# A graph attention layer: VectorE takes its V weights from SBUF, and the last sum moves to the last norm

## The chip, the cores and the metric

The kernel runs on one core of one Trainium2 chip. The metric is the device time of one execution in microseconds. Runs of this kernel lie within about 0.1% of each other; a change of 0.2% is about what a measurement can tell from none.

## The reference

4096 nodes with 512 features, 131072 edges with 8 biases each. One layer of attention along the edges, a feed-forward part, and a last norm over input plus layer:

```python
z = ln(x)*g1 + b1
q, k, v = z@Wq + bq, z@Wk + bk, z@Wv + bv          # 8 heads of 64
scores = (q[src] * k[dst]).sum(d) * scale + bias    # an edge and a head
alpha  = softmax of scores over the edges of one src
att    = sum over those edges of alpha * v[dst]
x1 = x + att @ Wo + bo
z  = ln(x1)*g2 + b2
y  = silu(z @ W1 + c1) @ W2 + c2                    # 512 -> 1024 -> 512
out = layernorm(x + x1 + y)
```

## The kernel before, in words

**First phase** (until about 1470 us): q, k, v are computed for all nodes and written to HBM, the edges are sorted into records by source node (GpSimd scatters 1024 times 128 records), and nodes are ranked by their number of edges. It isn't touched.

**Second phase.** 32 tiles of 128 nodes each, the nodes with most edges first. A tile's edges are worked off in groups of 8 slots: a slot holds one edge of each of the 128 nodes. A tile has 3 groups or more: most tiles have 5, later 4, the last ones 3, and there are 145 groups in all. In the code `stage` 0, 1 and 2 are the first three groups of a tile, stage 3 is every further one. A group goes so:

- GpSimd gathers K and V of its 8 slots from HBM with 8 indirect DMAs (L527, 512 KB each) into one of three buffers of the ring `region_a`. Before each pair of slots it waits until the weighting of that pair, three groups before, has released the buffer (`V_READY`). SyncE waits for the landings and passes them on (`LANDED`, L368).
- VectorE multiplies K by q, in four instructions of two slots (L1016, `products`); TensorE sums over d with transposes (L1356), ScalarE copies (L699), TensorE folds (L1364) into the scores.
- VectorE adds the bias, takes the running maximum and subtracts it (L1062 to L1066, `softmax`).
- ScalarE takes the exponents (`exponents`): L710 those of slots 2 to 5 into PSUM (`pv_ps`), L711 all of them into SBUF (`pr`).
- V is weighted: slots 2 to 5 by VectorE in two instructions (L1027, `weigh`), which read V from SBUF and the weights from `pv_ps`; slots 0, 1, 6 and 7 by ScalarE, a head at a time (L727). TensorE sums the weighted V with transposes (L1374), ScalarE copies (L705), TensorE turns that back into the accumulator (L1384), which VectorE scales (L1035).

VectorE weights group g after the products of group g+1, and ScalarE weights slots 6 and 7 of group g at the start of group g+1, ahead of that group's exponents.

Between the groups the tail of earlier tiles is woven in, in an order written out by hand. In tile t: in stage 0 VectorE adds the residual and norms tile t-2 (`middle`, L1114 to L1125), and TensorE computes the second feed-forward product of tile t-3 (`down`, L1423); in stage 1 VectorE adds that sum to the residual of tile t-3 (`take_y`, L1082), and TensorE does the first half of the first product of t-2 (`up`, L1415); in stage 2 VectorE takes the last norm of tile t-3 (`last_norm`, L1087 to L1094), TensorE the second half of `up` and the output projection (L1399) of tile t-1. Stage 0 also copies the new tile's q into PSUM (L1131). After the last tile the remaining steps are written out one after another.

PSUM has eight banks. `y_ps`, where `down` sums, is the first of the two banks of the hidden values (`h_ps[0]`), so `up` waits until `take_y` has emptied it:

```python
h_ps = bank[5:7]
y_ps, pv_ps = h_ps[0], bank[4][:, 0:(GROUP - 4) * HEADS].rearrange("p (s h) -> p s h", h=HEADS)
```

Each engine works off its own instructions in order; they meet by semaphores alone. GpSimd, VectorE, ScalarE, TensorE and SyncE each run their own loop over tiles and groups.

Of the kernel before, what the change touches and what calls it, by code (L numbers as in the profile page):

```python
# [36 lines left out]
def layer_kernel(nc, x, src, dst, edge_bias, Wq, bq, Wk, bk, Wv, bv, Wo, bo, ln1_g, ln1_b,  # L37
# [37 lines left out]
    with ExitStack() as ctx:  # L75
# [138 lines left out]
        qkv_ps = [bank[3], bank[4], bank[3]]  # L214
        scT_ps, sc_ps = bank[0][:, 0:2 * P], bank[0][:, 2 * P:2 * P + 2 * SH]
        vT_ps, acc_ps = bank[1], bank[7]
        wo_ps, q_ps = turn_ps, bank[3]
        h_ps = bank[5:7]
        y_ps, pv_ps = h_ps[0], bank[4][:, 0:(GROUP - 4) * HEADS].rearrange("p (s h) -> p s h", h=HEADS)

        names = """kv00 kv01 kv02 kv03 kv10 kv11 kv12 kv13 kv20 kv21 kv22 kv23 more_loaded rec_loaded src_loaded edges_loaded weights_loaded consts_a pad_ready
            table_cleared bias_cut bias_out bias_in hist_in hist_turned keys_ready turned turned_sb turned_out onehots_free onehots_ready hist_done prefix_in
# [399 lines left out]
        def _(act):  # L622
# [84 lines left out]
            def exponents():  # L707

                act.wait_ge(S["sc_ready"], now)
                act.activation(pv_ps, sc[:, 3:GROUP - 1, :], ACT.Exp)  # L710
                act.activation(pr[:, 0:GROUP + 1, :], sc[:, :, :], ACT.Exp).then_inc(S["p_ready"], 1)  # L711
                act.drain()

# [88 lines left out]
        def _(dve):  # L802
# [218 lines left out]
            def weigh():  # L1021

                kv_in = slots(was)
                dve.wait_ge(S["p_ready"], groups)
                for s in range(2, GROUP - 2, 2):
                    dve.wait_ge(SUMMED[s // 2], groups)
                    dve.tensor_tensor(vw[:, s:s + 2, :].rearrange("p s (h d) -> p s h d", h=HEADS),  # L1027
                                      kv_in[:, s:s + 2, C:2 * C].rearrange("p s (h d) -> p s h d", h=HEADS),
                                      pv_ps[:, s - 2:s, :].unsqueeze(3).broadcast_to([P, 2, HEADS, D]),
                                      ALU.mult).then_inc(V_READY[s // 2], 1)  # L1030

            def scale():
# [43 lines left out]
            def summed(reg):  # L1076
                return s_all[:, bass.ds(dve.snap(reg, min_val=0, max_val=C), C)]

            def take_y(k, s_w):

                dve.wait_ge(S["y_done"], k + 1)
                dve.tensor_tensor(s_w, s_w, y_ps[:, :], ALU.add).then_inc(S["y_taken"], 1)  # L1082
                dve.drain()

            def last_norm(u, s_w):

                dve.bn_stats(stats[:, :], s_w)  # L1087
                dve.drain()
                dve.bn_aggr(mv[:, 2:4], stats[:, :])
                dve.drain()  # L1090
                inverse_root(1)
                dve.tensor_copy(out_idx[:, :], row_all[:, u, 0].bitcast(I32))
                dve.tensor_scalar(s_w, s_w, mv[:, 2:3], rstd[:, 1:2], ALU.subtract, ALU.mult)
                dve.drain().then_inc(S["out_ready"], 1)  # L1094
# [33 lines left out]
            def body(t, stage):  # L1128
# [16 lines left out]
                    weigh()  # L1145
                    dve.tensor_copy(sc[:, 0, :], m_run[:, :])
                if stage == 1:
                    with dve.If(t > 2):
                        take_y(dve.snap(oldest), summed(dve.snap(dve.snap(q_at) * -1 + C)))
                    with dve.If(t > 0):  # L1150
                        finish(t)
                    first_weights()
                    dve.drain()
# [37 lines left out]
                if stage == 2:  # L1191
                    with dve.If(t > 2):
                        other = dve.snap(dve.snap(q_at) * -1 + C)
                        last_norm(bass.ds(dve.snap(nc.s_assert_within(t - 3, 0, NT - 4, skip_runtime_bounds_check_because="the If has t > 2")), 1),
                                  summed(other))
                    dve.nop()

# [15 lines left out]
            def half(u):  # L1213
                return s_all[:, (u % 2) * C:(u % 2 + 1) * C]
# [2 lines left out]
            middle(NT - 1)  # L1217
            hold(S["out_sent"], 16 * (NT - 3))
            residual(half(NT - 2))
            take_y(NT - 2, half(NT - 3))  # L1220
            dve.reg_add(groups, groups, 1)
            finish(NT)
            silu(NT - 1, 0)
            last_norm(slice(NT - 3, NT - 2), half(NT - 3))
            silu(NT - 1, 1)
            middle(NT)
            hold(S["out_sent"], 16 * (NT - 2))
            residual(half(NT - 1))
            take_y(NT - 1, half(NT - 2))
            last_norm(slice(NT - 2, NT - 1), half(NT - 2))  # L1230
            silu(NT, 0)
            silu(NT, 1)
            hold(S["out_sent"], 16 * (NT - 1))
            take_y(NT, half(NT - 1))
            last_norm(slice(NT - 1, NT), half(NT - 1))

        @block.tensor
        def _(pe):
# [169 lines left out]
            def up(k, a):  # L1408

                if a == 0:  # L1410
                    pe.wait_ge(S["z2_sb"], k)
                    pe.wait_ge(S["y_taken"], k)
                for m in range(a * HT // 2, (a + 1) * HT // 2):
                    for c in range(KT):
                        last = pe.matmul(h_ps[m // 4][:, (m % 4) * P:(m % 4 + 1) * P], W1_sb[:, c, m * P:(m + 1) * P],  # L1415
                                         z2T[:, c * P:(c + 1) * P], start=c == 0, stop=c == KT - 1)
                last.then_inc(H_DONE[a], 1)

            def down(k, a):

                pe.wait_ge(H_READY[a], k)
                for m in range(a * HT // 2, (a + 1) * HT // 2):
                    last = pe.matmul(y_ps[:, :], hT[:, m * P:(m + 1) * P], W2_sb[:, m, :], start=m == 0, stop=m == HT - 1)  # L1423
                if a == 1:
                    last.then_inc(S["y_done"], 1)
# [102 lines left out]
```

## Time and profile before

| what | value |
|---|---|
| median of 3 runs | 3608.19 us (3605.18 to 3608.59) |
| profiled execution | 3609.14 us, span 3607.4 us |
| PE busy | 2811.9 us (78%) |
| VectorE (DVE) busy | 2631.0 us (73%) |
| GpSimd (POOL) busy | 2342.4 us (65%) |
| ScalarE (ACT) busy | 1695.5 us (47%) |
| gathers L527 | 1160, 998 ns each |
| ScalarE's weighting L727 | 4640, 336 ns each |
| products L1016 | 580, 1216 ns each |
| VectorE's weighting L1027 | 290, 1213 ns each |

The share of busy time is a mean over phases with different limits; the time outside the second phase is 1470 of 3607 us. A gather's time on GpSimd is the time to issue it; its data lands later. In the timeline an "x4" row merges instructions of one kind that follow each other, and the bracket is the idle time of that engine ahead of the row with what ended it; "issue" there is time in which the engine waited for nothing that the profile shows.

### The profile page before, as it was taken

What the parts mean: (1) busy time and instruction counts of PE and PEld (TensorE: products, weight loads), DVE (VectorE), ACT (ScalarE), POOL (GpSimd) and SP (SyncE); (2) the same over time, 40 slices, a digit from 0 to 9 for tenths busy, and PEclk for the clock granted to TensorE, in tenths of its full rate; (3) what the DMA queues carried; (4) which work ended last, traced back from release to release, by engine and by line L of the source; (5) the groups of instructions that cost most, each with busy time, mean ns of one, the idle gap of its engine ahead of it and who ended that gap; (6) DMA issues with size and microseconds to landing.
All of it is one profiled execution on the core that took longest, in us unless ns stands there. A gap on an engine that the chain in (4) does not pass through costs nothing.

```text
span 3607.4 us, 82722 instructions
## 1 busy us (share of the span) xinstructions
PE 2811.9 (78%) x18693; PEld 2155.2 (60%) x18694; DVE 2631.0 (73%) x6460; ACT 1695.5 (47%) x6541; POOL 2342.4 (65%) x2549
## 2 busy tenths in 40 slices
PE   8665666666566666487888889988889898988997
PEld 7433333333333333377777777777777777777775
DVE  9777667767667766376777777777777777777874
ACT  0111111111111111286777777777777776777774
POOL 0477777777777777676666666666666666666650
PEclk5666666776667777698999999999999999999999
DMA  7323232323232222877888788788688888888770
GB/s 291 86 79 91 77 82 75 79 79 89 79 82 75 78 78 73 307 270 248 306 299 277 268 294 297 258 282 309 234 289 280 294 280 296 276 291 276 247 280 24
DMA packets 285668, 719.24 MB, mean 199 GB/s; under 512 B 86900, under 2 KB 103476, under 8 KB 285383
## 3 DMA queue, kind: packets, MB, share of 16 engines
q0 software_dynamic: 211776, 585.54, 47.3%
q1 hardware_dynamic: 73862, 133.41, 11.9%
q14 instruction: 23, 0.18, 0.0%
q8 instruction: 7, 0.11, 0.0%
HBM read 717.02 MB, written 72.97 MB: 219 GB/s over the span
## 4 chain that ended last, share of the span: by engine, by line
PE 36%; POOL 18%; issue 18%; DVE 8%; ACT 7%; DMA 6%; DVEq 3%; ACTq 2%; POOLq 1%; SPq 0%; PEld 0%; PEldq 0%
POOL records L410 17%; PE bank L1356 13%; ACT region_c L727 7%; PE wide L1415 6%; PE wide L1423 6%; DMA records<-region_c,pos_i 6%; PE bank L1399 3%; PE wide L1374 3%; DVE region_c L1016 2%; PE bank L1255 2%; PE wide L1384 2%; DVE region_c L964 1%; ACTq L727 1%; POOL region_a L527 1%; ACTq L766 1%
## 5 line engine op out<-in xcount | busy, mean ns | idle before, releaser
L527 POOL DMA_INDIRECT region_a<-kv,cols x1160 | 1157.8, 998 | 535.0 <-issue 434.0
L410 POOL DMA_INDIRECT records<-region_c,pos_i x1024 | 1010.8, 987 | 445.3 <-issue 412.7
L727 ACT ACTIVATE region_c<-region_a,pr 128x64 f32 x4640 | 1155.5, 336 | 44.0 <-issue 44.0
L1016 DVE TENSOR_TENSOR region_c<-region_a,bank 128x1024 f32<-128x1024 f32 x580 | 670.5, 1216 | 88.9 <-issue 61.0
L1356 PE MATMUL bank<-ident,region_c 128*128 128x128 f32 x4640 | 613.5, 289 | 129.9 <-DVE region_c L1016 124.9
L1356 PEld LDWEIGHTS bank<-ident,region_c 128*128 128x128 f32 x4640 | 584.5, 197 | 155.8 <-issue 150.0
L1374 PE MATMUL wide<-ident,region_c 128*128 128x128 f32 x4640 | 566.9, 275 | 78.0 <-ACT region_c L727 78.0
L1374 PEld LDWEIGHTS wide<-ident,region_c 128*128 128x128 f32 x4640 | 514.4, 144 | 111.9 <-ACT region_c L727 111.8
L649 ACT COPY region_c<-region_a 128x64 f32 x128 | 32.5, 254 | 1063.0 <-DMA records<-region_c,pos_i 1063.0
L1313 PE MATMUL bank<-region_b,region_a 128*128 128x512 f32 x768 | 490.7, 798 | 0.0
L1313 PEld LDWEIGHTS bank<-region_b,region_a 128*128 128x128 f32 x768 | 189.6, 260 | 253.3 <-issue 253.3
L1027 DVE TENSOR_TENSOR region_c<-region_a,bank 128x1024 f32<-128x1024 f32 x290 | 339.9, 1213 | 1.1 <-issue 1.1
L1300 PEld LDWEIGHTS wide<-region_c 64*128 64x128 f32 x2048 | 167.3, 241 | 239.9 <-issue 239.9
L928 DVE SCALAR_TENSOR_TENSOR region_c<-region_a,region_c 128x128 bf16<-128x128 int16 x1024 | 292.4, 349 | 24.1 <-issue 24.1
L1300 PE MATMUL wide<-region_c 64*128 64x64 f32 x2048 | 185.7, 335 | 152.4 <-issue 152.4
L699 ACT COPY region_c<-bank 128x256 f32<-128x256 f32 x145 | 54.0, 372 | 463.0 <-PE bank L1356 463.0
L1415 PE MATMUL wide<-region_c,region_b 128*128 128x128 f32 x2048 | 239.2, 275 | 3.2 <-ACT region_c L737 3.2
L1415 PEld LDWEIGHTS wide<-region_c,region_b 128*128 128x128 f32 x2048 | 233.6, 192 | 3.7 <-ACT region_c L737 3.7
L1423 PE MATMUL wide<-region_b,region_c 128*128 128x512 f32 x512 | 225.0, 592 | 0.0
L946 DVE TENSOR_TENSOR pos_i<-region_c 128x8 int32<-128x8 f32 x128 | 21.5, 168 | 271.1 <-DMA records<-region_c,pos_i 266.1
L1320 PE MATMUL bank<-ident,region_a 128*128 128x128 f32 x128 | 35.7, 434 | 228.2 <-DVE region_a L960 228.2
L1255 PE MATMUL bank<-region_c 128*64 128x64 bf16 x2048 | 180.3, 318 | 1.7 <-DVE region_c L847 0.7
(185 smaller groups left out, 3206.2 us busy)
## 6 DMA issues: line engine op xcount, KB each, us to landing
region_a<-srcT SPq DMA_DIRECT2D x128, 256.0 KB
region_a<-kv,cols POOLq DMA_INDIRECT x1160, 5.8
region_a<-hiT SPq DMA_DIRECT2D x256, 64.0 KB
records<-region_c,pos_i POOLq DMA_INDIRECT x1024
x_rows<-region_c SPq DMA_DIRECT2D x32, 512.0 KB
kv<-region_a SPq DMA_DIRECT2D x32, 512.0 KB
records<-region_c SPq DMA_DIRECT2D x32, 480.0 KB, 14.8
region_a<-in_x_dram SPq DMA_DIRECT2D x32, 256.0 KB
```

The costliest lines, as they stand in the source:

```text
L410: pool.indirect_dma_start(records, bass.IndirectOffsetOnAxis(ap=pos_i[j % 2][:, s:s + 1], axis=0), rec_w[j % 2][:, s, :], None).then_inc(S ...
L527: pool.indirect_dma_start(KV[r][:, s, :], None, kv, bass.IndirectOffsetOnAxis(ap=cols[r][:, s:s + 1], axis=0), bounds_check=L - 1, oob_is_ ...
L727: last = act.activation(vw[:, s, of], v_part[:, s, C + hd * D:C + (hd + 1) * D], ACT.Copy, scale=pr[:, s + 1, hd:hd + 1])
L928: last = dve.scalar_tensor_tensor(eq[:, s * P:(s + 1) * P], srcb[b][:, s * P:(s + 1) * P], src_f[:, bass.ds(st * STREAMS + s, 1)], tri[:, ...
L1016: last = dve.tensor_tensor(prods[:, of, :], kv_in[:, of, 0:C], q_ps[:, :].unsqueeze(1).broadcast_to([P, 2, C]), ALU.mult)
L1027: dve.tensor_tensor(vw[:, s:s + 2, :].rearrange("p s (h d) -> p s h d", h=HEADS), kv_in[:, s:s + 2, C:2 * C].rearrange("p s (h d) -> p s h ...
L1300: last = pe.matmul(wide_ps[b][:, side, s * LO:(s + 1) * LO], hitT[b][rows, s * P:(s + 1) * P], table_sb[rows, s * LO:(s + 1) * LO], start= ...
L1313: last = pe.matmul(qkv_ps[w][:, :], zT1[:, c * P:(c + 1) * P], Wqkv[:, w, c, :], start=False, stop=c == KT - 1)
L1356: last = pe.matmul(scT_ps[:, a * P:(a + 1) * P], prod_cols[:, i, a * SH:(a + 1) * SH], ident[:, :], start=i == 0, stop=i == D // FOLD - 1, ...
L1374: last = pe.matmul(vT_ps[:, c * P:(c + 1) * P], vw[:, s, c * P:(c + 1) * P], ident[:, :], start=s == 0 and c == 0, stop=s == GROUP - 1, is ...
L1415: last = pe.matmul(h_ps[m // 4][:, (m % 4) * P:(m % 4 + 1) * P], W1_sb[:, c, m * P:(m + 1) * P], z2T[:, c * P:(c + 1) * P], start=c == 0, ...
L1423: last = pe.matmul(y_ps[:, :], hT[:, m * P:(m + 1) * P], W2_sb[:, m, :], start=m == 0, stop=m == HT - 1)
```

## The change

VectorE's two weightings read their weights from `pr` in SBUF, as ScalarE does, and the exponent into PSUM is gone. The bank that held it becomes `y_ps`. `take_y` is no step of its own in stage 1 any more: its wait and its addition stand at the head of `last_norm` in stage 2. `up` no longer waits for `y_taken`; `down` does. In the steps after the last tile the addition likewise goes to the head of `last_norm`.

```diff
-        wo_ps, q_ps = turn_ps, bank[3]
+        wo_ps, q_ps, y_ps = turn_ps, bank[3], bank[4]
         h_ps = bank[5:7]
-        y_ps, pv_ps = h_ps[0], bank[4][:, 0:(GROUP - 4) * HEADS].rearrange("p (s h) -> p s h", h=HEADS)
...
                 act.wait_ge(S["sc_ready"], now)
-                act.activation(pv_ps, sc[:, 3:GROUP - 1, :], ACT.Exp)
                 act.activation(pr[:, 0:GROUP + 1, :], sc[:, :, :], ACT.Exp).then_inc(S["p_ready"], 1)
...
                                       kv_in[:, s:s + 2, C:2 * C].rearrange("p s (h d) -> p s h d", h=HEADS),
-                                      pv_ps[:, s - 2:s, :].unsqueeze(3).broadcast_to([P, 2, HEADS, D]),
+                                      pr[:, s + 1:s + 3, :].unsqueeze(3).broadcast_to([P, 2, HEADS, D]),
                                       ALU.mult).then_inc(V_READY[s // 2], 1)
...
-            def take_y(k, s_w):
+            def last_norm(k, u, s_w):
 
                 dve.wait_ge(S["y_done"], k + 1)
                 dve.tensor_tensor(s_w, s_w, y_ps[:, :], ALU.add).then_inc(S["y_taken"], 1)
                 dve.drain()
-
-            def last_norm(u, s_w):
-
                 dve.bn_stats(stats[:, :], s_w)
...
                 if stage == 1:
-                    with dve.If(t > 2):
-                        take_y(dve.snap(oldest), summed(dve.snap(dve.snap(q_at) * -1 + C)))
                     with dve.If(t > 0):
                         finish(t)
...
                 if stage == 2:
                     with dve.If(t > 2):
                         other = dve.snap(dve.snap(q_at) * -1 + C)
-                        last_norm(bass.ds(dve.snap(nc.s_assert_within(t - 3, 0, NT - 4, skip_runtime_bounds_check_because="the If has t > 2")), 1),
+                        last_norm(dve.snap(oldest), bass.ds(dve.snap(nc.s_assert_within(t - 3, 0, NT - 4, skip_runtime_bounds_check_because="the If has t > 2")), 1),
                                   summed(other))
...
             residual(half(NT - 2))
-            take_y(NT - 2, half(NT - 3))
             dve.reg_add(groups, groups, 1)
             finish(NT)
             silu(NT - 1, 0)
-            last_norm(slice(NT - 3, NT - 2), half(NT - 3))
+            last_norm(NT - 2, slice(NT - 3, NT - 2), half(NT - 3))
...
             def up(k, a):
                 if a == 0:
                     pe.wait_ge(S["z2_sb"], k)
-                    pe.wait_ge(S["y_taken"], k)
...
             def down(k, a):
                 pe.wait_ge(H_READY[a], k)
+                if a == 0:
+                    pe.wait_ge(S["y_taken"], k)
```

## Rows read from the trace of the kernel before

**Rows 1.** Windows: stretch, length, busy time of each engine, TensorE's granted clock, DMA share, GB/s.

```profile
1470.00:1655.00 185.00, 133.99 (x976) 122.51 (x977) 122.23 (x180) 117.70 (x471) 132.81 (x155) 0.87 0.80 297
...
2610.00:3490.00 880.00, 791.88 (x5821) 675.98 (x5819) 681.07 (x1270) 637.73 (x2501) 559.54 (x636) 1.00 0.81 281
```

**Rows 2.** Groups of GpSimd's instructions from 1469 to 1640 us, by line.

```profile
L527 POOL DMA_INDIRECT region_a<-kv,cols x111 | 110.4, 995 | 37.1 <-issue 30.3 <-POOL cols L505 6.2 <-ACT region_c L727 0.6
```

**Rows 3.** Chain of waits: start, length, what; DVEq is VectorE's sequencer.

```profile
1640.48 6.23 DMA region_a<-kv,cols
...
2216.37 0.21 DVEq L1178
...
3249.29 0.44 PE bank L1391 x4
...
3307.36 0.44 PE bank L1391 x4
...
3498.45 1.85 PE bank L1356 x16
```

**Rows 4.** VectorE's waits from 1480 to 1655, then 1700 to 2610: total, times, longest.

```profile
DVE region_c L1016 <- SPq L368: 18.4, 15, 3.6
...
DVE region_c L1016 <- SPq L368: 0.3, 1, 0.3
```

**Rows 5.** Single lines, duration min/median/max in ns; L1027 from 1490 to 1640 us.

```profile
L1027 DVE TENSOR_TENSOR region_c<-region_a,bank x24: 1210/1212/1216, 1497.9 to 1632.8; 128x1024 f32<-128x1024 f32 x24
...
L1125 DVE TENSOR_TENSOR region_c<-region_c x32: 673/685/757, 1658.1 to 3576.1; 128x512 f32 x30, 128x512 f32<-128x512 f32 x2
...
L710 ACT ACTIVATE bank<-sc x145: 201/202/203, 1492.6 to 3537.0; 128x32 f32<-128x32 f32 x145
```

**Rows 6.** Timeline, start, length, engine, where VectorE's instructions meet GpSimd's, and one weighting.

```profile
2650.04 0.68 DVE L1125 TENSOR_TENSOR region_c<-region_c 128x512 f32 x1
2650.10 1.48 POOL L527 DMA_INDIRECT region_a<-kv,cols  x1 [0.30 <-issue]
...
2165.37 1.18 POOL L527 DMA_INDIRECT region_a<-kv,cols  x1 [0.16 <-issue]
2165.57 0.69 DVE L1125 TENSOR_TENSOR region_c<-region_c 128x512 f32 x1
...
1066.61 0.35 DVE L928 SCALAR_TENSOR_TENSOR region_c<-region_a,region_c 128x128 bf16<-128x128 int16 x1
1066.74 1.06 POOL L410 DMA_INDIRECT records<-region_c,pos_i  x1 [0.30 <-issue]
...
1066.89 0.35 DVE L928 SCALAR_TENSOR_TENSOR region_c<-region_a,region_c 128x128 bf16<-128x128 int16 x1
...
3265.96 2.34 DVE L1027 TENSOR_TENSOR region_c<-region_a,bank 128x1024 f32<-128x1024 f32 x2
```

**Rows 7.** TensorE's waits from 1700 to 2610 us.

```profile
PE wide L1384 <- ACT region_c L705: 3.2, 13, 0.3
```

**Rows 8.** Timeline of a second group's end: VectorE's products, TensorE's next transposes.

```profile
3243.70 4.61 DVE L1016 TENSOR_TENSOR region_c<-region_a,bank 128x1024 f32<-128x1024 f32 x4 [0.34 <-issue]
...
3249.57 1.97 PE L1356 MATMUL bank<-ident,region_c 128*128 128x128 f32 x16
```

**Rows 9.** VectorE's timeline: the last addition, and L1062 of a fourth and a fifth group.

```profile
3593.85 0.69 DVE L1082 TENSOR_TENSOR region_c<-region_c,wide 128x512 f32<-128x512 f32 x1 [4.00 <-PE wide L1423]
3594.63 0.69 DVE L1087 BATCH_NORM_STATS2 stats<-region_c 128x6 f32<-128x512 f32 x1
...
3271.46 0.23 DVE L1062 TENSOR_TENSOR sc<-bank,region_c 128x64 f32<-128x64 f32 x1 [1.90 <-PE bank L1364]
...
2216.91 0.22 DVE L1062 TENSOR_TENSOR sc<-bank,region_c 128x64 f32<-128x64 f32 x1 [1.18 <-PE bank L1364]
```

**Rows 10.** Timeline behind the third and last group of a tile: the next tile's products.

```profile
3495.75 4.62 DVE L1016 TENSOR_TENSOR region_c<-region_a,bank 128x1024 f32<-128x1024 f32 x4 [0.33 <-issue]
```

More of the change, by code:

```diff
@@ L1228, in _ @@
             residual(half(NT - 1))
-            take_y(NT - 1, half(NT - 2))
-            last_norm(slice(NT - 2, NT - 1), half(NT - 2))
+            last_norm(NT - 1, slice(NT - 2, NT - 1), half(NT - 2))
             silu(NT, 0)
@@ L1233, in _ @@
             hold(S["out_sent"], 16 * (NT - 1))
-            take_y(NT, half(NT - 1))
-            last_norm(slice(NT - 1, NT), half(NT - 1))
+            last_norm(NT, slice(NT - 1, NT), half(NT - 1))
         @block.tensor
```

## The prediction, made before the result

> **What bounds the kernel now.** I read by stages first, then the chain of waits, then who waits for whom, then the timeline of single groups. By stages [rows 1]: until about 1470 us the first phase runs, which the change doesn't touch. From 2610 to 3490 us TensorE is busy 792 of 880 us, GpSimd 560. Between 1470 and 1655 us it is the other way: TensorE 134 of 185 us, GpSimd 133 us, and GpSimd is really fuller than that, because between two of its gathers lie 0.30 us of issue. Its row for 1469 to 1640 us [rows 2] has 111 gathers of 995 ns and 37.1 us of idle time before them, nearly all "issue" and its own index copies, 0.6 us for anybody else. So in this stretch GpSimd works without a pause. The chain agrees: it leaves it by the landing of the last gather at 1640.48 us, 6.23 us long [rows 3], and VectorE waits there 18.4 us in 15 pieces for SyncE's word that data landed; from 1700 to 2610 us the same wait is 0.3 us once [rows 4]. After about 1660 us the chain is TensorE's, with a piece of ScalarE's weighting in each group and one of VectorE's at a tile's start. I therefore treat two regimes: twelve groups that hang on GpSimd, and some 130 that hang on TensorE, with GpSimd ahead by the ring of three buffers.
>
> **Part 1: VectorE's two V weightings (L1027) read both inputs from SBUF.** Their own length: now 1212 ns each with the weights in PSUM. The rows nearest in kind, at half the width, are L1125 with both inputs in SBUF, 685 ns [rows 5], and L1082 with one in PSUM, 0.69 us [rows 9]: no difference to speak of, at most 0.01 us either way, 0.02 at full width. I take 0.
>
> What it does to GpSimd is the larger matter. While VectorE's L1125 ran from 2650.04 to 2650.72, a gather issued at 2650.10 took 1.48 instead of 0.99 us: it ended 0.86 us after VectorE did [rows 6]. A plain gather thus seems to need something of SBUF 0.12 us after its start, and gets it only when a VectorE instruction with two SBUF inputs is over. The reverse isn't so: L1125 at 2165.57 began inside a gather and took its usual 0.69 us [rows 6]. And between two such VectorE instructions back to back GpSimd gets in: of the run of L928, the one at 1066.61 ended at 1066.96; a scatter issued at 1066.74 ended at 1067.80, again 0.84 us after that end, although the next L928 had begun at 1066.89 and ran until 1067.24 [rows 6].
> So I price one pair of weightings, which takes 2.34 us together [rows 6], so W1 from 0 to 1.21 and W2 from 1.13 to 2.34, against gathers 1.30 us apart. A gather that starts at 0.05 to 1.09 (0.80 of the cases) is held until 1.09, mean 0.52 us, and the next starts at 2.39, free again. One that starts at 1.09 to 1.30 (0.16) is held by W2 until 2.22, mean 1.03 us. In the rest (0.04) the next one meets W2, 0.9 us. Together 0.42 + 0.16 + 0.04 = 0.62 us a group. GpSimd's stretch has 24 instructions L1027, 12 pairs [rows 5]: 12 x 0.62 = 7.4 us, all on the path, since GpSimd has no pause there that could take it up and VectorE already waits for it. Bounds: 0, if the hold falls on transfers that are late anyway; 18.5 us, if W1 and W2 hold it as one (until 2.22 from any start in 0.05 to 1.30: 1.55 us x 12). I take 7.4.
> In the later groups the same 0.62 us comes off GpSimd's lead. A late tile of four groups takes 3249.29 to 3307.36, 58.07 us [rows 3], so the 880 us hold 61 groups; GpSimd's 320 us without work [rows 1] are 5.3 us a group, of which 8 x 0.30 = 2.4 are issue; of the 2.9 left some is issue for the tile's own transfers, but 1.55 fits too. Term: 0. If that cover were gone, each group would pay.
>
> The Trainium skill, "SBUF — State Buffer", section "SBUF: two separate sides", says that VectorE and GpSimd share a pair of ports under an exclusive lock, held for the whole instruction, which VectorE also takes with two SBUF inputs against a GpSimd operation that reads SBUF, and that whoever comes second is blocked fully. The 1.48 us row agrees for GpSimd as the second; the 2165.57 row doesn't for VectorE as the second. By the rule in full the sum would be that of the third rival.
>
> **Part 2: one exponent less on ScalarE.** L710 takes 202 ns [rows 5], in front of L711; so each group's weights are ready at most 0.2 us earlier. ScalarE's piece on the chain is the weighting of slots 6 and 7 of the group before, which comes ahead of the exponents, so it isn't shortened. What could gain is the copy L705 behind them: TensorE waits for it 3.2 us in 13 places [rows 7], where VectorE's own chain of that group is as late. 0, at best -2.6 us (13 x 0.2).
>
> **Part 3: the last sum.** Its bank is new, so no wait of `up` for `y_taken` is left; in the middle of the run the addition precedes even the group's softmax, `up` comes after its sums: nothing. `down` now waits for `y_taken`, a whole tile later than the norm: nothing. The addition moves on VectorE from the second group of a tile to the third. In the second group it frees 0.68 to 0.8 us before the softmax; but the products that follow it start at 3243.70 and are half done (two of four in 4.61 us) at 3246.0, and TensorE, busy with the feed-forward, asks for them at 3249.57 [rows 8]: 0.
>
> In the third group it adds: the step from addition to statistics is 3593.85 to 3594.63, 0.78 us, and register steps for the wait, for which I take 0.1 to 0.2 (L1178, a few such steps, is 0.21 [rows 3]): 0.94 us. The fourth group begins that much later. Where does this meet TensorE? VectorE next waits at L1062 for TensorE's scores. Before the L1062 of a fourth group VectorE is idle 1.90 us; before that of a fifth, to which the chain leads through VectorE's own steps and not through the scores, 1.18 us [rows 9], of which 0.21 is a branch (L1178) that the fourth group doesn't take [rows 3]. The slack is 1.90 - 1.18 + 0.21 = 0.93 us, and without the branch's allowance 0.72. So 0.94 against 0.93: I take 0 and keep (0.94 - 0.72) x 29 tiles = 6.4 us as the upper end; behind that wait VectorE's chain leads straight to the next tile's products, for which TensorE waits, so an overrun counts fully.
> Where a tile has only three groups, the products of the next follow the norm directly: they start at 3495.75, are half done 2.3 us later at 3498.1, and TensorE takes them at 3498.45, after its output projection [rows 3, 10]. Slack 0.35, so 0.94 - 0.35 = 0.6 us, once. At the end of the kernel the last addition is the same link as before: 0.
>
> **Sum.** 7.4 + 0 + 0 + 0.6 = 8.0 us. The profiled execution took 3609.1 us (span 3607.4), 0.95 above the median 3608.2 of the runs; 3609.1 + 8.0 = 3617.1 for such an execution, 3616 for the median.
>
> **Rivals.**
> - GpSimd's holds don't reach the end: its early gathers run at 297 GB/s with the transfers' engines at 0.80 [rows 1], so a late issue could meet a shorter queue and land as before. For it: the last landing takes 6.2 us. Against: the engines are no fuller than later (0.81), where GpSimd leads. 3608.2 + 0.6 = 3609 us.
> - VectorE overruns in the fourth group. Place L1062; it decides once the moved steps exceed the slack. 3616 + 6.4 = 3622 us.
> - The hold is coarser than I read it: W1 and W2 act as one (18.5 in place of 7.4: 3627), or VectorE too waits for the rest of a gather, 0.76 x 0.5 = 0.38 us a group on its path where the slack is used up, 29 x 0.38 = 11 us: also 3627 us. The full rule of the skill named above is this second form.
> - Faster: the second group of a tile hangs on VectorE, not TensorE, and the addition's leaving opens it by 0.78 us in 29 tiles: 3608 - 22.6 = 3586 us. Against: the 3.5 us between products and TensorE's start [rows 8]; it would decide only below that. A smaller gain, part 2's 2.6 us without the holds, is 3606.
>
> **Chances.** Forecast 0.48, holds without effect 0.24, overrun 0.13, coarser hold 0.07, small gain 0.04, large gain 0.04. A measurement tells about 0.2% from no change, 7.2 us: 3615.4 and above is slower, 3601.0 and below faster. Of the forecast a little over half lies above that line (its own spread is 3611 to 3621), of the overrun and the coarse hold all: slower 0.50, same 0.44, faster 0.06. Range 3607 to 3626.
>
> **What would show it.** Gathers L527 of 1.1 to 2.0 us beside L1027 in all groups, about 0.6 us a group in sum (some 90 us in GpSimd's busy time); the chain's landing at 1640.48 moved to about 1648; the same 58.1 us for late tiles. Wrong would be: L527's mean still 998 ns; a longer late tile (then it is VectorE's fourth group); L1027 longer than 1.25 us.

## The result

| | before | changed |
|---|---|---|
| median | 3608.59 us (3603.21 to 3617.57, 11 runs) | 3617.59 us (3614.56 to 3621.53, 11 runs) |
| profiled execution | 3609.14 us, span 3607.4 us | 3617.59 us, span 3615.8 us |

The ratio is 1.0024, with a 95% interval of 1.0015 to 1.0032: slower by 9.0 us, where 3616 us (7.8 above the 3608.2 of the runs known then) was forecast. A second comparison (experiment 5) gave 3617.00 against 3607.57 us, ratio 1.0026 (1.0016 to 1.0037).

In what follows I go through the profile of the changed kernel in the order of the rows of before. In its text the gathers are L526 (L527 before), the products L1014 (L1016), VectorE's weighting L1025 (L1027), the moved addition L1080 (L1082), the sums over d L1346 (L1356), GpSimd's copies of the edge indices that its gathers read L504 (L505). Of the 32 tiles the first three have 7, 6 and 6 groups, twelve have 5, fifteen have 4 and the last two 3; that most have 5, as said ahead, is not so.

First the windows, which answer to [rows 1]:

```profile
1470.00:1655.00 185.00, 130.33 (x928) 118.62 (x928) 115.51 (x168) 111.65 (x439) 134.95 (x147) 0.86 0.77 278
2610.00:3490.00 880.00, 792.03 (x5824) 676.28 (x5823) 682.78 (x1267) 631.60 (x2443) 592.09 (x634) 1.00 0.80 278
```

In the same 185 us TensorE, VectorE and ScalarE each did some 4 to 7 us less, GpSimd was busy 2.1 us more with 8 instructions fewer. In the 880 us of late tiles TensorE did what it did before (792.03 against 791.88), while GpSimd's busy time grew by 32.5 us without any effect on TensorE. That is the picture of two regimes: GpSimd's longer instructions cost time where it has no lead, and none where it has.

GpSimd's gathers and index copies of the first stretch (answers to [rows 2]; the window ends 8 us later, at 1648 us, so that it holds as many gathers); the index copies of the kernel before in its own window; and all gathers of the changed kernel, minimum, median and maximum:

```profile
L526 POOL DMA_INDIRECT region_a<-kv,cols x111 | 116.9, 1053 | 37.1 <-issue 30.7 <-POOL cols L504 6.3
L504 POOL COPY cols<-region_c 128x8 int32 x15 | 5.0, 335 | 8.2 <-ACT region_c L725 7.1 <-issue 1.1
...
L505 POOL COPY cols<-region_c 128x8 int32 x15 | 2.9, 196 | 8.4 <-issue 8.4
...
L526 POOL DMA_INDIRECT region_a<-kv,cols x1160: 984/992/2055, 1470.1 to 3517.8; - x194
```

The same 111 gathers take 116.9 instead of 110.4 us; the idle time ahead of them is 37.1 us both times. The median is 992 ns (990 before): most gathers are untouched, and a few are twice as long. Only the mean of the line shows it, and only a little. The 15 index copies take 5.0 instead of 2.9 us: they are held too, which the prediction had not thought of.

The chain of waits [rows 3] (start, length, what):

```profile
1648.97 6.14 DMA region_a<-kv,cols
...
3256.80 0.44 PE bank L1381 x4
...
3314.87 0.44 PE bank L1381 x4
```

It leaves GpSimd at 1648.97 instead of 1640.48 us. The late tile goes from 3256.80 to 3314.87, 58.07 us as before, and 7.51 us later than before. Behind the first of the two tiles of three groups TensorE takes the next tile's products at 3506.79 instead of 3498.45, 8.34 us later. The span ends 8.4 us later. So 7.5 us come ahead of the late tiles, 0.8 us in this tile of three groups, and next to nothing after.

VectorE's waits from 1480 to 1655 us [rows 4] and its weighting [rows 5] (duration minimum, median, maximum):

```profile
DVE region_c L1014 <- SPq L367: 30.0, 22, 4.7
...
L1025 DVE TENSOR_TENSOR region_c<-region_a,pr x290: 1214/1217/1277, 1498.1 to 3551.5; 128x1024 f32<-128x1024 f32 x145
```

VectorE now waits 30.0 us for landings in place of 18.4. Its weighting is as long as before (1217 against 1212 ns) and is never held: its longest is 1277 ns, and of the 162 weightings that begin while GpSimd issues a DMA the longest takes 1224 ns.

How a gather and, earlier in the trace, an index copy are held (timeline: start, length, engine, and in brackets the idle time of the engine ahead of it):

```profile
1611.08 0.99 POOL L526 DMA_INDIRECT region_a<-kv,cols  x1 [0.30 <-issue]
1611.78 2.35 DVE L1025 TENSOR_TENSOR region_c<-region_a,pr 128x1024 f32<-128x1024 f32 x2
...
1612.37 1.49 POOL L526 DMA_INDIRECT region_a<-kv,cols  x1 [0.30 <-issue]
...
1533.49 2.35 DVE L1025 TENSOR_TENSOR region_c<-region_a,pr 128x1024 f32<-128x1024 f32 x2
...
1535.17 0.73 POOL L504 COPY cols<-region_c 128x8 int32 x1 [3.60 <-ACT region_c L725]
```

The first weighting ends at 1612.99, the gather at 1613.86, 0.87 us later, although the second weighting runs until 1614.13. This is what the prediction had read from other pairs of instructions [rows 6]. The index copy, 0.20 us at other times, takes 0.73 and ends at 1535.90, 0.05 us after the second weighting of its pair.

I also followed the gathers one by one through the two traces. The first starts 0.08 us later than before and the first of the 14th group 7.43 us later, so 7.35 us arise in the first 13 groups (tiles 0 and 1). GpSimd's own instructions account for all of it: in this stretch its gathers take 5.5 us more (108.9 against 103.4), its 13 index copies 2.1 us more (4.6 against 2.6), and it stands idle 0.2 us less. In the 14th group one more us is lost, in a gather, and the last gather of that group starts 8.49 us late. In the second profiled execution of the changed kernel the first 13 groups lose 7.77 - 0.49 = 7.3 us, 5.8 of it in gathers and 1.7 in index copies.

The way from there to the late tiles is less even. By the copies of q, one at each tile's start, tiles 3 to 16 start 4.7 to 8.0 us later than before in the first profile of the changed kernel and 8.0 to 9.7 us in the second, and only from tile 17 on are these differences constant, 7.5 and 7.0 us. I have one trace of the kernel before and don't know what moves the middle tiles.

### The profile page after: what moved, and what is told of

Same layout as the page of the kernel before. It is cut to its first block, busy times and chain, and to the rows that moved or that the text cites. A ratio compares the mean times of both kernels' runs of the same rounds, so it can differ in the third digit from the quotient of the medians.

```text
span 3615.8 us, 82487 instructions
## 1 busy us (share of the span) xinstructions
PE 2811.7 (78%) x18693; PEld 2152.7 (60%) x18694; DVE 2629.2 (73%) x6460; ACT 1678.5 (46%) x6396; POOL 2413.6 (67%) x2549
## 4 chain that ended last, share of the span: by engine, by line
PE 35%; POOL 21%; issue 19%; ACT 7%; DVE 6%; DMA 6%; DVEq 2%; ACTq 2%; POOLq 1%; PEld 0%; PEldq 0%; SPq 0%
POOL records L409 19%; PE bank L1346 12%; ACT region_c L725 7%; PE bank L1414 6%; PE wide L1404 6%; DMA records<-region_c,pos_i 6%; PE bank L1389 3%; PE wide L1364 3%; PE bank L1245 2%; DVE region_c L1014 2%; POOL region_a L526 2%; PE wide L1374 2%; ACTq L725 1%; ACTq L764 1%; DVE bank L1126 1%
## 5 line engine op out<-in xcount | busy, mean ns | idle before, releaser
L526 POOL DMA_INDIRECT region_a<-kv,cols x1160 | 1208.2, 1042 | 522.6 <-issue 412.9
L1014 DVE TENSOR_TENSOR region_c<-region_a,bank 128x1024 f32<-128x1024 f32 x580 | 670.8, 1215 | 101.7 <-issue 59.6
L1346 PE MATMUL bank<-ident,region_c 128*128 128x128 f32 x4640 | 614.2, 289 | 140.9 <-DVE region_c L1014 140.8
L1346 PEld LDWEIGHTS bank<-ident,region_c 128*128 128x128 f32 x4640 | 584.6, 197 | 167.8 <-issue 157.3
L648 ACT COPY region_c<-region_a 128x64 f32 x128 | 32.5, 254 | 1065.7 <-DMA records<-region_c,pos_i 1065.7
L1025 DVE TENSOR_TENSOR region_c<-region_a,pr 128x1024 f32<-128x1024 f32 x290 | 341.4, 1218 | 1.1 <-issue 1.1
L1414 PE MATMUL bank<-region_b,region_c 128*128 128x512 f32 x512 | 225.0, 592 | 0.0
```

The costliest lines, as they stand in the source:

```text
L526: pool.indirect_dma_start(KV[r][:, s, :], None, kv, bass.IndirectOffsetOnAxis(ap=cols[r][:, s:s + 1], axis=0), bounds_check=L - 1, oob_is_ ...
L1014: last = dve.tensor_tensor(prods[:, of, :], kv_in[:, of, 0:C], q_ps[:, :].unsqueeze(1).broadcast_to([P, 2, C]), ALU.mult)
L1346: last = pe.matmul(scT_ps[:, a * P:(a + 1) * P], prod_cols[:, i, a * SH:(a + 1) * SH], ident[:, :], start=i == 0, stop=i == D // FOLD - 1, ...
```

## The experiments

**What has to be known of the chips first.** The first ten of the twelve runs fell on three chips that run every kernel 23 to 24% slower, the kernel before too: 4488, 4434 and 4479 us. Single instructions are as long as ever there (products 1216 ns, gathers 1.00 to 1.02 us), but the engines stand still between them. One of the waits of a kernel with parts 1 and 2 alone on such a chip (engine, waiting line, what for: total us, times, longest):

```profile
POOL region_a L527 <- issue: 751.9, 1103, 7.3
```

In the kernel before at ordinary speed this row is 434.0 us with a longest wait of 4.3 us. Gaps of over 3 us between two GpSimd instructions, those of its sequencer counted too, number 107 there and 9 at ordinary speed; in VectorE 179 and 34. I don't know their cause. What matters: in tiles 0 and 1, where the changed kernel loses its time at ordinary speed, GpSimd has pauses there, and the runs of one kernel spread by 0.5 to 1.5%. A whole time can't show 8 us there; which gathers are held can still be read.

**1. Parts 1 and 2 alone.**

```diff
-                act.activation(pv_ps, sc[:, 3:GROUP - 1, :], ACT.Exp)
...
-                                      pv_ps[:, s - 2:s, :].unsqueeze(3).broadcast_to([P, 2, HEADS, D]),
+                                      pr[:, s + 1:s + 3, :].unsqueeze(3).broadcast_to([P, 2, HEADS, D]),
```

> The kernel before with VectorE's V weights from SBUF and one exponent (parts 1 and 2); the last sum keeps its place and bank (part 3 undone). Theory: GpSimd's gathers are held behind VectorE's weightings, and that reaches the end only in the first 13 groups, where GpSimd has no pause: +7 to +9 us against before, so 3616 to 3618, gathers' mean about 1.04 us. Rival A, that the moved addition made the 9 us: the same as before, 3608 to 3610. Rival B, holds that cost in all groups: also +8, with the early stretch no later than 1 us.

> Before with parts 1 and 2 alone: VectorE's two V weightings read their weights from SBUF, one exponent per group; the last feed-forward sum stays where it was, in the second group. Theory (gathers held in the first 13 groups): tile 3 starts about 7.7 us later than before, the last tile of three groups keeps its 46.6 us, whole time +7 to +8 us. Rival A (the moved addition makes the 9 us): tile 3 starts as before, whole time +0. Rival B (a slot of the addition in the second group had hidden part of the holds): tile 3 starts more than 9 us later.

**2. SBUF weights only in the first two tiles, or only after them** (the kernel before; VectorE's weighting stands in both branches of an If on the tile, and both exponents are computed).

```diff
-            def weigh():
+            def weigh(t=None, stage=3):
...
+                with dve.If(t < (3 if stage == 0 else 2)):
+                    weigh_from(early_weights)
+                with dve.Else():
+                    weigh_from(late_weights)
```

> The kernel before, with both exponents kept, but VectorE takes the V weights of the first two tiles (13 groups) from SBUF, of the other 30 tiles from PSUM; a branch on VectorE in each group chooses. Theory: the whole cost sits there, +7 to +9 us against before, 3616 to 3618, and the start of tile 2 (1638.6 us before) comes 7 to 8 us later. Rival B, cost spread over all groups: 13 of 145 of 9 us, +0.8 us. Rival A: 0. The branch, if it isn't hidden, up to 0.1 us a group, the same in the next kernel.

> The mirror image: V weights of the first two tiles from PSUM, of the other 30 from SBUF, both exponents kept, the same branch. Theory: GpSimd's lead takes up the holds, -1 to +2 us against before, 3608 to 3611, though the gathers are just as long in the later tiles (about 43 us of the 50 in sum). Rival B: +8 us. Rival A: 0 (this kernel doesn't tell A from the theory, the one before does).

**3. The changed kernel with PSUM weights in tiles 0 and 1**, the same If, and for these tiles the second exponent.

```diff
+                with act.If(t < 2):
+                    act.wait_ge(S["sc_ready"], now)
+                    act.activation(pv_ps, sc[:, 3:GROUP - 1, :], ACT.Exp)
```

> The changed kernel with the second exponent and the PSUM weights back for the first two tiles alone, in the bank that the last sum uses from tile 3 on. Theory: it takes back the holds that count: 7 to 9 us under the changed kernel, 3609 to 3611, equal to before within 2 us, and the start of tile 2 is back at about 1638.7 us. Rival A: nothing comes back, 3617. Rival B: 0.8 us come back.

> The changed kernel, but in the first two tiles VectorE's weightings take their weights from PSUM, with an exponent of their own for them; from the third tile on all is as in the changed kernel. Theory (only holds that fall where GpSimd has no lead cost anything): tile 3 starts within 1 us of before's 1733.7 us, the tile of three groups takes 47.7 us, whole time +0.5 to +1.5 us over before. Rival (holds cost in every group, or the move of the addition costs in every tile): +5 us or more. The mean gather L526 falls only a little, to some 1037 ns from 1042.

> The changed kernel with PSUM weights in the first two tiles, once more. On the chips of the first two sets all kernels took some 4430 to 4490 us, and in tiles 0 and 1 only 2 to 4 gathers fell on a weighting instead of 10, so 7 us of holds could not be seen in a time. If this chip runs the kernel before at some 3608 us: theory (the changed kernel's 9 us are 7.4 of gathers held in the first tiles, 1 of the tile of three groups, the rest unexplained): tile 3 starts at 1734 to 1735 us, whole time +0.5 to +1.5 us, ratio 1.000 to 1.0005. Rival (the moved addition or later holds make the 9 us): ratio 1.0015 or more. If it runs it at 4400 us or more: ratio 0.997 to 1.002 by either, and no weighting with PSUM weights coincides with a gather longer than 1.05 us, while those with SBUF weights coincide with gathers up to 2.0 us.

Measured in 1 to 3, all on the slow chips; "held" is the longest gather in tiles 0 and 1. One of the twelve executions behind the first row took 8479.75 us; the ratio leaves it out, and without it the median is 4486.77.

| kernel | weights in tiles 0, 1 | median | ratio to before, 95% | held |
|---|---|---|---|---|
| parts 1 and 2 | SBUF | 4490.69 | 0.9996 (0.9973 to 1.0019) | 1.82 us |
| the same again | SBUF | 4440.91 | 1.0007 (0.9977 to 1.0037) | 2.03 us |
| SBUF in tiles 0, 1 only | SBUF | 4503.54 | 1.0022 (0.9996 to 1.0048) | 2.00 us |
| SBUF from tile 2 on | PSUM | 4486.83 | 1.0009 (0.9987 to 1.0031) | 1.05 us |
| changed, PSUM in tiles 0, 1 | PSUM | 4478.18 | 0.9973 (0.9955 to 0.9990) | 1.04 us |
| the same again | PSUM | 4427.89 | 0.9984 (0.9962 to 1.0006) | 1.05 us |
| the same, third | PSUM | 4469.22 | 0.9974 (0.9947 to 1.0001) | 1.04 us |

The gathers of tiles 0 and 1 for the first row of the table, and for the fifth; then those of the fifth from tile 2 on (duration minimum, median, maximum):

```profile
L527 POOL DMA_INDIRECT region_a<-kv,cols x118: 987/993/1821, 1872.6 to 2100.4; - x118
```

```profile
L527 POOL DMA_INDIRECT region_a<-kv,cols x115: 984/990/1038, 1879.9 to 2099.3; - x115
...
L527 POOL DMA_INDIRECT region_a<-kv,cols x1040: 984/990/2066, 2112.4 to 4388.0; - x174
```

Within one kernel the maximum goes from 1.04 to 2.07 us at the tile from which on the weights come from SBUF. That part 1 holds the gathers is thereby shown by taking it away and putting it back. What it costs in time isn't: only 2 to 5 gathers of tiles 0 and 1 were held there, in place of the 9 and 10 of the two profiles at ordinary speed; GpSimd's pauses are the likely reason. From the first products to tile 3 the four profiled kernels with SBUF weights in tiles 0 and 1 (the one of experiment 4 among them) took 319 to 335 us, mean 326, the six with PSUM weights 318 to 326, mean 321.5: the sign is that of the theory, but the spread is larger than the difference. Inconclusive.

The changed kernel with PSUM weights at first came out 0.16 to 0.27% below before three times (one of the three intervals excludes 1), which no theory had. It has no step of its own for the addition any more, and VectorE's gaps of over 2.5 us in the second phase (from 1850 us) number 85 to 96 in its three traces against 89 and 102 with parts 1 and 2 alone. That saving a step saves some standing time on such a chip is an idea, not shown: the counts overlap.

**4. The free bank used for a second q.** If a tile's start hangs on the copy of q, the next q can be copied a group earlier, into the bank that part 1 frees; the last sum stays where it was. The cuts show the copy; the products read the bank whose turn it is.

```diff
-                if stage == 0:
-                    hold(S["q_loaded"], t * 16 + 16)
-                    dve.tensor_copy(q_ps[:, :], row_q[:, bass.ds(dve.snap(q_at, min_val=0, max_val=C), C)])
-                    dve.drain()
...
                 if stage == 2:
+                    with dve.If(t < NT - 1):
+                        q_next = dve.snap(dve.snap(q_at) * -1 + C, min_val=0, max_val=C)
+                        hold(S["q_loaded"], t * 16 + 32)
+                        dve.tensor_copy(q_wide[:, bass.ds(q_next, C)], row_q[:, bass.ds(q_next, C)])
+                    dve.nop()
                     scale()
```

> Before with parts 1 and 2; the bank that became free holds a second q, so that the next tile's q is copied into it in the third group, ahead of the scaling, and the copy of 0.69 us with its wait leaves the start of a tile, where the products and then TensorE wait for it. The last sum stays in the second group. Theory (a tile's start hangs on VectorE's copy and products, about 1 us in each of some 29 tiles, paid back once in the third group where there is slack): late tiles of four groups 57.1 instead of 58.07 us, whole time -30 + 8 = -22 us, near 3586. Rival (the copy only moves the wait, the third group has no room for it): late tiles still 58.1 us, whole time +8 us.

> The same with the double bank for q, but in the first two tiles VectorE's weights come from PSUM (the first bank of the hidden values, which is free then) with an exponent of their own. Theory: the 7 to 8 us of held gathers are saved on top of the tile starts: whole time -30 us, near 3578, and 7 to 8 us below the version with SBUF weights throughout. Rival (the 8 us would be made up later when tiles are shorter): no difference between the two.

> The double bank for q with PSUM weights in the first two tiles, once more. On a chip that runs the kernel before at some 3608 us: theory: late tiles of four groups 57.1 in place of 58.07 us, whole time 3575 to 3585 us, ratio 0.991 to 0.994. Rival (the copy's place moves the wait into the third group): late tiles 58.1 us, ratio 1.000. On a chip at 4400 us or more: ratio 0.994 to 1.000, as the first time (0.9971).

Measured: 4445.42 us, ratio 0.9995 (0.9969 to 1.0022); with PSUM weights in tiles 0 and 1 4427.19, 0.9971 (0.9943 to 1.0000), and 4465.58, 0.9964 (0.9938 to 0.9990). The mean late tile took 71.1, 71.1 and 71.4 us in them, and 69.3 to 71.0 in the seven profiles of experiments 1 to 3 (mean of tiles 17 to 28): no microsecond a tile was saved, so that expectation fell on these chips. The 0.3 to 0.4% of the last two can't be told from the 0.16 to 0.27% that experiment 3 has without the second q. At ordinary speed this kernel was not measured, and whether it beats both there stays open.

**5. The changed kernel itself, once more.**

> The changed kernel itself, on a chip that may run everything some 24% slower, as those of the last sets did. There only 2 to 4 gathers of the first two tiles fell on a weighting, so that GpSimd's holds have little place to cost in. Theory (the 9 us of the first measurement are holds where GpSimd sets the pace): where the kernel before takes some 4430 to 4490 us, the changed one is not slower by 9 us; ratio 0.996 to 1.001, like that with PSUM weights in the first two tiles (0.9973, 0.9984, 0.9974). Rival (the moved addition or a hold in every group makes them): ratio 1.002 or more here too. At 3608 us for before: ratio 1.0024 by both.

This set fell on a chip at ordinary speed: 3617.00 us (3614.34 to 3619.37, 8 runs) against 3607.57, ratio 1.0026 (1.0016 to 1.0037). The span is 3615.3 us, the chain leaves GpSimd at 1648.26 us, late tiles take 58.07 us, and the first one of three groups 47.7 (46.6 before). So the loss and its two places repeat. The question for which it was run, whether the changed kernel loses nothing on a slow chip, was not answered.

**6. The disputed cost by itself.** On the same chip as 5: GpSimd gathers without any wait (128 rows of 256 bytes each), VectorE alternates copies inside PSUM (their length changes, so that the meeting points do too) and a weighting, in three ways. Of the code only VectorE's loop is shown, which runs once in each of the three stretches (`part`).

```python
                for n in range(WEIGHTINGS):
                    for to, w in enumerate((512, 512, 512, FILL[n % 8])):
                        dve.tensor_copy(fill[to][:, 0:w], fill[4][:, 0:w])
                    if part == 2:
                        last = weigh(0, 4, pr[:, :, :])
                    else:
                        for at in (0, 2):
                            pv_w = pv[:, at * HEADS:(at + 2) * HEADS].rearrange("p (s h) -> p s h", h=HEADS)
                            last = weigh(at, 2, pv_w if part == 0 else pr[:, at:at + 2, :])
...
```

> No layer is computed: three stretches of 120 gathers of 128 rows each on GpSimd, without waits, while VectorE does 24 times some filling copies inside PSUM (2 to 3 us, of changing length) and a weighting of 4 slots: first in two instructions with PSUM weights, then in two with SBUF weights, then in one instruction with SBUF weights. Theory (a gather is held from 0.12 us after its start until the VectorE instruction is over, GpSimd gets in between two of them): first stretch 0.99 us a gather, nowhere over 1.05; second: 0.6 us a weighting more, so 24 x 0.62 = 15 us more for the 120 gathers, less where the lengths happen to fall in step; third: one instruction of 2.3 us holds from any start in it: (2.3 / 1.29) starts per weighting of which one is held, for 1.0 to 1.5 us on the mean, 24 to 36 us more, single gathers up to 3.1 us. Rival (the two act as one): second stretch as the third. Rival (no lock, only slower): gathers 1.1 to 1.3 us throughout, none over 1.5. VectorE's weightings keep 1.21 us in all three (2.4 for the long one); by a lock against both they would show up to 1.9 us.

GpSimd's gathers and VectorE's weightings of the three stretches, each with its own window:

```profile
L53 POOL DMA_INDIRECT kv<-in_x_dram,cols x120 | 119.6, 997 | 39.9 <-issue 39.9
L67 DVE TENSOR_TENSOR vw<-v_in,pv 128x1024 f32<-128x1024 f32 x48 | 56.1, 1209 | 0.0
...
L53 POOL DMA_INDIRECT kv<-in_x_dram,cols x120 | 134.9, 1124 | 39.4 <-issue 39.4
L67 DVE TENSOR_TENSOR vw<-v_in,pr 128x1024 f32<-128x1024 f32 x48 | 56.4, 1215 | 0.0
...
L53 POOL DMA_INDIRECT kv<-in_x_dram,cols x120 | 161.8, 1348 | 39.3 <-issue 39.3
L67 DVE TENSOR_TENSOR vw<-v_in,pr 128x2048 f32<-128x2048 f32 x24 | 54.9, 2286 | 0.0
```

VectorE's 24 rounds last 108 us of each stretch, so some 80 of the 120 gathers run beside them. With PSUM weights and copies inside PSUM a gather takes 997 ns, and none but the first of all (1.13 us) over 1.05. With SBUF weights the 120 gathers take 15.3 us more, 0.64 us for each of the 24 pairs, where the prediction had 0.62. As one instruction of the same work it is 42.2 us more, 1.76 us each, where I had expected 1.0 to 1.5. Two pieces of the timeline, one of each stretch:

```profile
193.56 2.35 DVE L67 TENSOR_TENSOR vw<-v_in,pr 128x1024 f32<-128x1024 f32 x2
194.18 1.46 POOL L53 DMA_INDIRECT kv<-in_x_dram,cols  x1 [0.30 <-issue]
...
399.19 2.28 DVE L67 TENSOR_TENSOR vw<-v_in,pr 128x2048 f32<-128x2048 f32 x1
399.26 3.08 POOL L53 DMA_INDIRECT kv<-in_x_dram,cols  x1 [0.30 <-issue]
```

In both stretches exactly one gather was held per pair or long weighting, 24 of 120, and the held ones end 0.86 to 0.87 us after the VectorE instruction in the way: the pair lets GpSimd in after its first half, the long one only at its end. "The two act as one" fell, and so did "only slower, no lock". VectorE's 1209, 1215 and 2286 ns show no trace of waiting, and its 24 rounds take 108.3 us with PSUM weights and 108.5 with SBUF weights, so the hold is one-sided.

The price depends on where the gathers start, and these starts were not spread evenly. In the second stretch all 24 began 0.20 to 0.85 us after their pair did and were held by its first half, none by the second; the prediction had starts from 0.05 to 1.30, a sixth of them held by the second half. That 0.64 and 0.62 agree so closely is therefore in part luck.

## Why the prediction was right, point by point

- **Two regimes.** Held: the late tiles of four groups last 58.07 us before and after, and GpSimd's 32.5 us more in the window from 2610 us cost nothing.
- **Part 1, VectorE's own duration, 0.** Held: 1217 against 1212 ns, over 48 instructions of the experiment 1215 against 1209.
- **Part 1, GpSimd, +7.4 us.** The mechanism held and the sum came out, the sum with some luck. The 12 pairs of the stretch held gathers for 6.5 us, 0.54 us a pair, and for 5.8 us in the second profile, 0.49 a pair: less than 0.62. What the prediction had at nothing without saying so are GpSimd's index copies, held for 2.1 and 1.7 us. Together, with 0.2 us less of idle time, that is 8.4 and 7.3 us at the last gather of the stretch, and 7.5 and 7.0 us at the late tiles. The prediction's bounds of 0 and 18.5 are excluded: the loss is there twice, GpSimd gets in between the two weightings each time, and a coarse hold measured alone costs 1.76 us. That the held instructions make the loss of GpSimd's stretch rests on this account of the trace, in which nothing else has grown. To take them away at ordinary speed and see the time return was what experiment 3 was for; its three runs fell on slow chips. So the cause is located and its price measured, but the return of the time is not shown.
- **Part 1, later groups: 0.62 us each, some 90 us in GpSimd's busy time.** This was mis-sized: L526 grew by 50.4 us over all groups (1208.2 against 1157.8), 0.35 us a group, and by 46.4 in the second profile. The 0.62 supposes that gathers meet weightings at any phase. That is so while GpSimd runs freely; once it leads by the whole ring, it waits for the weighting that frees a buffer (41 times, 69.8 us in all), and its phase is set by VectorE. In four successive late groups (the 124th to the 127th) the held gathers' time beyond 0.99 us was 0.00, 0.00, 0.96 and 0.23 us; from the 100th on it was 0.00, 0.14, 0.96 and 0.25. Of the 88 gathers that a weighting held after 1649 us, 64 began at one of three distances from its pair's start: 0.86 to 0.90, 1.25 to 1.30, or 2.08 to 2.09 us. The forecast time was not touched by it, since the term was covered.
- **Part 2, 0.** Held, and for the reason given. From 1700 to 2610 us TensorE's 13 waits for the copy L705 (3.2 us, [rows 7]) have no row of their own any more, but in the same window its waits for VectorE's products went from 33.0 us (L1016) to 36.1 us (L1014), 14 times each: VectorE's chain was as late. The tiles got no shorter. Part 3 changed VectorE's order in the same kernel, so these two numbers are not part 2's alone.
- **Part 3, second and fourth group, 0.** Held: products behind the second group start some 0.9 us earlier relative to the tile, those of the fourth group 0.9 us later, and the tile is 58.07 us. The slack of 0.93 us, which I had as good as used up, sufficed.
- **Part 3, the tile of three groups, +0.6 us.** Right in place, a little small. The rows of the changed kernel (the chain; then the timelines of VectorE and TensorE) show why:

```profile
3496.02 0.27 DVEq L1080
3496.54 0.69 DVE region_c L1080
3497.37 0.69 DVE stats L1082
...
3504.29 4.61 DVE L1014 TENSOR_TENSOR region_c<-region_a,bank 128x1024 f32<-128x1024 f32 x4 [0.33 <-issue]
...
3506.79 2.05 PE L1346 MATMUL bank<-ident,region_c 128*128 128x128 f32 x16 [0.84 <-DVE region_c L1014]
```

  From addition to statistics it is 0.83 us (0.78 in [rows 9]), and the register steps ahead of it take 0.27, for which I had 0.1 to 0.2. VectorE gets 1.04 us later in this tile, where I had 0.94, TensorE 0.83, and it now waits 0.84 us for the products, where it had been the later one before. The slack was mis-sized too: TensorE starts 2.50 us after the products do (3504.29 to 3506.79), not 2.3, so that of the time from 3495.75 to 3498.45 in the kernel before 0.20 us was slack, not 0.35. The second profile has 0.9 us here.
- **The row of one-sidedness.** L1125 at 2165.57 [rows 6] did take its usual 0.69 us, but the gather beside it took 1.18 us, which the prediction passed over. It ended 0.89 us after L1121, a TENSOR_SCALAR of VectorE that had begun at 2165.11 and taken 0.55 us: that one had held it. The conclusion stands on the 162 weightings and on experiment 6.
- **Sum.** 8.0 forecast, 8.4 by the profiled spans, 9.0 by the medians, whose own interval is 5.4 to 11.5 us. Of the rivals, "holds without effect" (3609) is excluded by the ratio, the overrun in the fourth group (3622) by the 58.07 us, the coarser hold by experiment 6, the faster ones by the ratio. In the chances one step doesn't add up: 0.50 for slower needs 0.30 of the forecast's 0.48 above the line, which is more than "a little over half"; with a little over half it is some 0.46.

The Trainium skill's rule for the shared ports ("SBUF — State Buffer", section "SBUF: two separate sides") was weighed in the prediction against one row for each side. The 72 measured weightings with SBUF weights agree with it for GpSimd as the second (held until VectorE's instruction is over), and don't for VectorE as the second: 1215 ns where gathers run all the time, against 1209 with PSUM weights.

## What to carry to other kernels

Two SBUF inputs on VectorE, in place of one in SBUF and one in PSUM, can be free for VectorE and still be paid by GpSimd: count how many of its DMA issues, and of its copies from SBUF, start within such an instruction, and price them only in stretches where GpSimd sets the pace. Where that can't be avoided, several short VectorE instructions hold it less than a long one (0.64 against 1.76 us for the same work). A bank of PSUM that is freed at such a price should buy a wait that is on the chain; here the waits that went had never been late.

## What the runs showed of the hardware that I had not expected

- How exact the hold is: all 48 held gathers of experiment 6 ended 0.864 to 0.873 us after the end of the VectorE instruction that held them, whatever their start. A free gather takes 0.99 us, so the step that is held stands some 0.12 us after its start (0.99 - 0.87, an estimate), and what follows takes its full time afterwards. An index copy of GpSimd ends 0.05 us after the instruction that held it.
- Two SBUF tensors are not the only way to hold GpSimd. In the kernel before 18 gathers take over 1.06 us. Three of them end 0.87 to 0.89 us after L1125, but 14 end 0.86 to 0.90 us after L1093 or L1121, VectorE's scaling step of a norm, which reads one SBUF tensor and two columns (`mv`, `rstd`), writes SBUF and takes 0.55 us.
- Copies of VectorE inside PSUM (693 ns each for 128x512) beside a gather cost the gather nothing to speak of: 997 ns on the mean.
- Three chips ran the same kernel 23 to 24% slower than it ran elsewhere (4434 to 4488 against 3608 us), with instructions of unchanged length and many more gaps of over 3 us between them. There a change worth 8 us can't be timed.
